# Graph attention on one core: who fetches the target slices of a chunk, SP's transfers or ACT's copies

## What is computed

```python
xn = layernorm(x)
x = x + gnn(xn, edges) + mix(xn)
x = x + ffn(layernorm(x))       # 8 experts, top 2
# gnn: two layers of graph attention (4 heads of 128, then 1 head of 256)
logits = leaky_relu(al_s[src] + al_d[dst], 0.2)
e = exp(logits - segment_max(logits, dst)[dst])
alpha = e / segment_sum(e, dst)[dst]
out = segment_sum(h[src] * alpha, dst)
```

## Time and profile before

| | |
|---|---|
| timed runs, median of 3 | 5681.7 us (5672.57 to 5684.13) |
| span of the profiled execution | 6588.7 us; the profile gives no other time of that execution |
| mean granted TensorE clock in it | 0.821 |
| busy: PE, DVE, ACT, POOL | 71%, 47%, 43%, 55% of the span |
| first walk, from its first gather to its last | 182.7 to 2789.5 us |
| second walk | 3008.1 to 5555.6 us |

### The profile page before, as it was taken

How to read it: one execution, slowest core, us unless ns; L and a number is a source line. 1 busy time by engine, 2 the same in 40 slices (tenths; PEclk the granted TensorE clock), 3 DMA queues, 4 the chain that set the end, 5 groups by cost and what they waited for, 6 DMA issues and landing times. The chain is left out here.

```text
span 6588.7 us, 83150 instructions
## 1 busy us (share of the span) xinstructions
PE 4647.1 (71%) x21069; PEld 3510.5 (53%) x21069; DVE 3112.7 (47%) x8587; ACT 2835.5 (43%) x8419; POOL 3631.1 (55%) x3778
## 2 busy tenths in 40 slices
PE   7477777777777777773555565665555556699999
PEld 4355555555555555652444444443343444588887
DVE  4365666656656666662444444444444444711111
ACT  2455655655555556673334334333232223322222
POOL 0565666656655666545666666666666664244443
PEclk9698888888888888896777777777777777699999
DMA  5676777777777777633444444444455553644332
GB/s 190 193 203 196 201 200 199 202 195 203 201 196 199 203 197 202 191 116 102 118 115 116 119 114 116 118 115 116 118 136 139 139 135 107 203 157 131 125 133 79
DMA packets 703586, 1027.53 MB, mean 156 GB/s; under 512 B 391738, under 2 KB 483736, under 8 KB 702862
## 3 DMA queue, kind: packets, MB, share of 16 engines
q0 software_dynamic: 229312, 718.64, 39.2%
q1 hardware_dynamic: 473246, 302.52, 15.9%
q10 hardware_dynamic: 560, 1.05, 0.1%
HBM read 951.81 MB, written 65.48 MB: 154 GB/s over the span
## 5 line engine op out<-in xcount | busy, mean ns | idle before, releaser
L861 POOL DMA_INDIRECT walk_ring<-s_h,walk_index x3320 | 3170.3, 955 | 2120.8 <-issue 1004.3
L1022 PE MATMUL walk_pM<-walk_ring,walk_hit 128*128 128x262 f32 (+1 forms) x9960 | 3017.1, 455 | 235.2 <-issue 133.4
L1022 PEld LDWEIGHTS walk_pM<-walk_ring,walk_hit 128*128 128x128 f32 x9960 | 2150.5, 225 | 789.7 <-issue 385.3
L886 ACT ACTIVATE walk_ring<-walk_ring 128x128 f32<-128x128 f32 (+1 forms) x6640 | 2140.9, 414 | 30.2 <-issue 24.3
L1252 DVE TENSOR_TENSOR acc<-walk_pM,acc 128x520 f32 (+1 forms) x1494 | 833.6, 558 | 1834.2 <-remote 1040.8
L876 ACT ACTIVATE walk_ring<-walk_gap 128x40 f32<-128x40 f32 (+1 forms) x249 | 54.0, 258 | 2549.6 <-DVE walk_gap L1214 1867.9
L926 PE MATMUL walk_pC<-all_ident,walk_best 128*84 128x128 f32 (+1 forms) x166 | 57.7, 348 | 857.5 <-DVE walk_best L1170 552.7
L1219 DVE TENSOR_TENSOR walk_hit<-walk_pK,walk_meta 128x512 f32<-128x512 f32 x830 | 560.9, 676 | 11.8
L926 PEld LDWEIGHTS walk_pC<-all_ident,walk_best 128*84 128x84 f32 (+1 forms) x166 | 19.8, 119 | 925.0 <-issue 924.9
L2050 ACT ACTIVATE expert_hT<-expert_pH,expert_b 128x256 f32<-128x256 f32 x448 | 187.6, 470 | 595.2 <-PE expert_pH L2101 595.2
L2101 PE MATMUL expert_pH<-expert_xT,expert_w 128*128 128x256 f32 x1792 | 397.8, 380 | 1.7 <-issue 1.7
(11 more groups left out here) (319 smaller groups left out, 4119.1 us busy)
## 6 DMA issues: line engine op xcount, KB each, us to landing
walk_hitT<-s_places SPq DMA_DIRECT2D x166, 640.0 KB
expert_w<-in_fw_dram SPq DMA_DIRECT2D x56, 1024.0 KB
walk_ring<-s_h,walk_index POOLq DMA_INDIRECT x3320
walk_goal<-walk_target SPq DMA_DIRECT2D x830, 6.0 KB
walk_goal<-walk_target SPq DMA_DIRECT2D x830, 1.5 KB
walk_xk<-s_xT SPq DMA_DIRECT2D x98, 128.0 KB
walk_resets<-s_resets SPq DMA_DIRECT2D x415, 20.0 KB
down<-in_fw_dram SPq DMA_DIRECT2D x8, 1024.0 KB, 11.9
```

Of the source, the lines that this page charges most:

```text
L861: pool.indirect_dma_start(ring[:, r % RS, t, :], None, table, bass.IndirectOffsetOnAxis(ap=index[:, r % TS, t:t + 1], axis=0)).then_inc(ro ...
L886: last = nc.scalar.activation(row, row, ACT.Copy, scale=ring[:, r % RS, t, at + FH:at + FH + 1])
L1022: last = nc.tensor.matmul(pM[:, b, a, 0:WIDE], hit[:, (r * CGROUPS + g) % HBUF, t % GROUP, :], ring[:, r % RS, t, a * HALF_ROW:a * HALF_RO ...
```

## The change

`load_goals` and its calls leave SP. ACT gets `goals`, with the same wait for the tables, the reading of ten registers, and ten copies inside SBUF in place of the DMAs; since `goal` is a single buffer, it also waits for the spread of chunk n - 1, as SP did ahead of the places. It is called after the ten scalings of chunk c for chunk c + 2, ahead of `roots` and of the next weights, and for chunks 0 and 1 after the filling of `acc`, ahead of the first weights. PE's wait counts one per chunk in place of 160.

```diff
-                def load_goals(n, i, r):
-                    sp.wait_ge(tables_in[r % IS], tables_of(i, r))
-                    sp.sem_inc(part_seen, 1)
-                    at = windows_of(mybir.EngineType.SP, r)
-                    for s in range(CS):
-                        sp.dma_start(goal[:, s, :, :], target[:, at[s], :, :]).then_inc(goals_in, 16)
...
-                load_goals(0, 0, 0)
                 sp.wait_ge(spread_out, 1)
                 load_places(1)
-                load_goals(1, 0, 1)
...
                     sp.wait_ge(spread_out, c + 2)
                     load_places(c + 2)
-                    load_goals(c + 2, (c + 2) // TURN, (c + 2) % TURN)
...
+                def goals(n, i, r):
+                    act.wait_ge(tables_in[r % IS], tables_of(i, r))
+                    if n >= 1:
+                        act.wait_ge(spread_out, n)
+                    act.sem_inc(part_seen, 1)
+                    at = windows_of(mybir.EngineType.Activation, r)
+                    for s in range(CS):
+                        last = nc.scalar.copy(goal[:, s, :, :], target[:, at[s], :, :])
+                    last.then_inc(goals_in, 1)
...
                     for s in range(CS):
                         scale(c, i, r, s)
+                    if c + 2 < CHUNKS:
+                        goals(c + 2, (c + 2) // TURN, (c + 2) % TURN)
                     if mixing and 1 <= c <= NT:
                         roots(c - 1)
...
+                act.wait_ge(cleared, 1)
+                goals(0, 0, 0)
+                goals(1, 0, 1)
                 weights(0, 0, 0)
                 loop(chunk)(act)
...
-                    pe.wait_ge(goals_in, (n + 1) * (16 * CS))
+                    pe.wait_ge(goals_in, n + 1)
```

## The result

The changed kernel takes 5668.98 us (median of 20 runs, 5661.24 to 5677.35), the kernel before 5678.83 us (median of 20, 5662.19 to 5687.15): ratio 0.9982, 95% interval 0.9975 to 0.9989. That is 9.85 us or 0.18% less: a gain the runs can tell from nothing, but still, only just, inside the 0.2% that the prediction called "same".

The account below looks back on a forecast made before the run. POOL's gather issue, 25.0 us a chunk, was taken as the bound, with a floor of 5581.9 us. All terms summed to 0 against the timed median 5681.7, giving 5680 us, with an 8-in-10 range of 5610 to 5790.

Parts of the forecast that it names:

- case A: Whole kernel: no change, since POOL's gather issue covers the added ACT work and the loop; 5680 us, 5668 to 5692, chance 0.42.
- POOL's issue sets the walks: Both walks: 20 gathers 1.25 us apart make 25.0 us a chunk; timed median only 99.8 us above the floor.
- is stretched by something of its own: Profiled execution: its span, 907 us above the timed median, was taken as peculiar to that execution, not the timed runs.
- PE's results seem to be signalled late while gathers are in flight: Walks: PE's readers start late, DVE idling 4.93 and 4.33 us in a mixing chunk; taken as the profiled execution's stretch.
- The sum for the profiled execution: Profiled run after the change: DVE waits 3.1 us in 49 mixing chunks, 150 us, giving a span near 6740 us.
- ACT's ten copies: ACT, every chunk: ten small copies at 0.19 us each, 1.9 us a chunk (1.5 to 2.9).
- DVE's new wait: Walk two's 49 mixing chunks: DVE waits 1.7 us (1.1 to 3.1) for ACT's square; costed 0, covered by POOL's 25.0.
- rival S: Walk two's 49 mixing chunks: the loop, not POOL, sets them, so DVE's wait costs +83 us, 5765 us; chance 0.32.
- SP's 6.2 us a chunk: SP, every chunk: one register load and ten transfers removed, 1.11 + 10 × 0.51 us; costed at 0 inside the walks.
- The starts: First chunks of the walks: goals come earlier in walk two; costed at 0, at best some 14 us.
- Rival F: Both walks: fewer small packets recover part of the 99.8 us lost to DMA contention or late signals; half is 5632, chance 0.21.
- The estimate of 6.8 us of engine time a chunk: DMA engines: ten transfers at the skill page's 0.68 us; noted as disagreeing with 3.66 us for SP's whole queue.

Follow-up runs that it names:

- extra_gather2: The changed kernel with a 21st gather of 32 B rows per chunk, result unused; 5840.97 us, 1.0280 of the kernel before, on a first-kind chip.
- group 1: The first four follow-up kernels, run on one chip beside the kernel before, which took 6591.93 us there (median of 25 runs).
- roots_first: The changed kernel with ACT's roots moved ahead of its ten copies in the mixing chunks; 5668.52 us, 0.9981 of the kernel before.
- dummy_both2: The changed kernel with SP still issuing ten transfers a chunk, 12 B a partition, into a spare tile; 5682.13 us, 1.0004 of the kernel before.
- before_again: The kernel before, unchanged, run again for its trace on a first-kind chip; 5681.38 us, ratio 1.0000.
- group 5: The changed kernel run again on a second-kind chip; 6566.65 us against 6660.15 for the kernel before, ratio 0.9856.
- extra_gather: The changed kernel with a 21st gather of 32 B rows per chunk, result unused; 6705.86 us, 1.0171 of the kernel before, on a second-kind chip.
- copies_x5: The changed kernel with four small extra ACT copies for each of the ten, 40 more a chunk; 6592.39 us, 1.0010 of the kernel before.

## Why the prediction was right, and where it wasn't

The time (5680 forecast, 5669 measured, at the lower end of case A's own 5668 to 5692) came true, and so did a change under 0.2%, and case A in that POOL's issue sets the walks. By steps:

- **POOL's issue sets the walks, 1.25 us x 20 a chunk.** Shown by extra_gather2: 102.1 of 103.8 us in walk two. The 99.8 us over the floor were forecast from the median alone; the trace of the kernel before on the first kind has them: 76.7 + 28.1 = 104.8 us of pauses.
- **The profiled execution "is stretched by something of its own".** This step failed. The stretch isn't that execution's: the three times shown are like those of the first kind of chip and the profile like those of the second, where all 25 runs of group 1 took as long. For the same reason "PE's results seem to be signalled late while gathers are in flight" is true of the second kind alone.
- **The sum for the profiled execution, 6740 us, failed** twice: that run was of the first kind (5672.7 us), and on the second the changed kernel is at 0.9856 of before and not at 1.02. The term that was mis-sized is DVE's 3.1 us in 49 chunks (77.8 us in 36 measured), and the change's gain there, 94 us, was costed at 0.
- **ACT's ten copies, 1.9 us (1.5 to 2.9).** 1.15 us measured (191.7 / 166), under the lower end: in a row they follow each other every 0.11 us. The single copy lasts 196 ns, near the 0.19 taken; the error was to line up durations that overlap.
- **DVE's new wait, 1.7 us without late signals.** The group grows from 54.0 to 135.5 us over 49 chunks, 1.66 us each. Taking it away again (roots_first) gains nothing, so "POOL's 25.0 covers it: 0 us" is shown, and rival S has fallen for the first kind.
- **SP's 6.2 us a chunk.** SP's wait for the gap grew by 2884.3 - 1478.8 = 1405.5 us over 162 chunks, 8.7 us each (the load's wait included): more than forecast. It was forecast to be worth nothing; whether it has a part in the 10 us stays open, as dummy_both2 gives SP this work back together with the packets.
- **The starts.** PE's wait for the goals goes from 65.1 to 51.9 us; the gain from earlier goals was costed at "0, at best 14 us". dummy_both2 has the early goals and not the gain: 0.
- **Rival F in small.** Taking the transfers away is what gives the 10 us, as F had it, at a tenth of its bound of 99.8 us, and the term that stood for it in the sum was 0. That it works by DMA contention, as F said, isn't shown. Its other half, late signals in small, falls: no wait of these traces is "remote". So case A is right within its 0.2%, and with the wrong reason for the part under it; at 0.18% that was close. On the second kind F's ratio would have been the better forecast. The estimate of 6.8 us of engine time a chunk for the ten transfers, by the Trainium skill (DMA: Bandwidth & Descriptors, section Bandwidth), isn't borne out: SP's queue gave up 18.5% - 16.2% = 2.3% of the span (44.4% and 44.0% for the gathers' own), 131 us or 0.8 a chunk. The step that failed is the use of the figure: that page of the Trainium skill gives 0.68 us for 4 KB brought from HBM by GpSimd, as the floor of 64 packets at about 10.5 ns, and not as a price of every small transfer. Here 239040 packets over 16 engines took 131 us, 8.8 ns each.

The last point rests on the queues of before_again's page:

```profile
DMA packets 703586, 1027.53 MB, mean 181 GB/s; under 512 B 391738, under 2 KB 483736, under 8 KB 702862
...
q0 software_dynamic: 229312, 718.64, 44.4%
q1 hardware_dynamic: 473246, 302.52, 18.5%
```

The packets that went, 473246 - 234206 = 239040 or 144 a transfer, are half of that queue's and an eighth of its time.

## What to carry to other kernels

Compare the span of a profile with the timed runs before reading it. When they differ by 16%, the profile may be of another chip and its waits not those of the timed runs; profile the kernel again before building a theory on them. A change that moves work off an engine that isn't the bound is worth what it takes out of the bound's way, here 0.18%; but elsewhere the same change can be worth eight times that (1.44% in group 5), so a small gain of this sort is worth keeping. To show what binds, add a known amount to it: one gather a chunk returned nearly its full 1.25 us in walk two. And run the kernel that an experiment starts from beside it: extra_gather and copies_x5 ran in group 1 without the changed kernel, and beside the kernel before alone they say little.

## What the runs showed of the hardware

- The five groups ran on five different chips, and these fall into two kinds: 5678 and 5679 us for the kernel before (groups 2 and 3; the result's runs are like them), and 6592, 6639 and 6660 (groups 1, 4, 5), with the profile of before at 6588.7. Operations of ACT and POOL last equally long on both; PE's products take 455 ns in the mean on the second and 431 on the first. What PE makes is seen late on the second: 252 waits of DVE ahead of its adds have no releaser that the profile finds, 4.1 us each and 8.9 at most, and 227 of POOL 2.6 us each. Nearly all of the difference falls in the walks: before the first gather the two traces of the kernel before differ by 2.0 us, behind the last by 10.1 (1033.1 and 1023.0). No run here tells the cause, nor whether it is the chip or something else that went with the group.
- On the second kind ten transfers a chunk from one partition, of 12 packets each, came with a longer time (1.0321) than ten from 128 partitions, of 144 packets (1.0025, on another chip). The cause is open.
- A gather is issued every 1.2507 us without SP's small transfers and every 1.2527 with them, in six traces of the first kind. Whether it is the traffic or something laid down with the program wasn't settled.
- Ten copies of 6 values a partition with the source's place from a register ran in 1.10 us on ACT:

```profile
3023.64 1.10 ACT L877 COPY walk_goal<-walk_target 128x6 bf16 x10 [0.22 <-issue]
3024.65 0.59 ACT L893 ACTIVATE walk_square<-walk_pKV 128x512 f32<-128x512 f32 x1
3025.28 0.69 DVE L1091 TENSOR_REDUCE walk_ssum<-walk_square 128x8 f32<-128x512 f32 x1 [2.73 <-ACT walk_square L893]
```

This is a mixing chunk, later in the walk than that of the earlier trace rows, as the changed kernel has it on the first kind: copies, square, sum, with DVE idle for 2.73 us behind ACT. Chunks 5 to 50 of that walk take 25.24 us each all the same.
